# Splitting the scaling of the second exponentials between VectorE and GpSimd in a differential attention kernel

## The reference

```
Q1, Q2, K1, K2 = halves (64 columns each) of xn @ Wq + bq and xn @ Wk + bk
A1 = Q1 @ K1.T / 8;  A2 = Q2 @ K2.T / 8
P  = softmax(A1) - lam * softmax(A2)        # rows over 1024 keys
O  = P @ V;  Y = concat(O) @ Wo + bo;  layer norm of Y, times 0.2
```

## Time and profile before

| what | value |
|---|---|
| median of 3 runs | 1190.11 us (1189.4 to 1190.41) |
| the profiled execution | 1192.49 us |
| its span, first to last instruction | 1190.7 us |
| mean granted clock of PE | 0.987 |
| busy PE, DVE, ACT, POOL | 95%, 76%, 80%, 83% of the span |
| steps of attention | 256, in 32 items of 8 |

### The profile page before, as it was taken

One profiled execution on the slowest core, in us unless ns is written; L12 is line 12 of the kernel. 1 busy time (PEld: TensorE's weight loads), 2 busy tenths in 40 slices (PEclk: granted clock), 3 DMA queues, 4 the chain that ended last, 5 costly groups with the idle time before them and its releaser, 6 DMA issues.

```text
span 1190.7 us, 27816 instructions
## 1 busy us (share of the span) xinstructions
PE 1135.0 (95%) x9730; PEld 767.3 (64%) x9730; DVE 904.9 (76%) x1573; ACT 952.0 (80%) x1711; POOL 986.1 (83%) x609
## 2 busy tenths in 40 slices
PE   5899999999999999999999999999999999997998
PEld 4666666666666666666666666666666666664797
DVE  8778888888888888888887888888888878873510
ACT  3288888988888988888988888888889888884432
POOL 3599999999999999989888999999989888898000
PEclk9899999999999999999999999999999999997999
DMA  8842122222211222222222211122222221100000
GB/s 202 331 113 62 47 61 61 61 61 61 60 43 38 58 61 55 55 66 55 55 45 54 55 45 32 45 55 55 55 55 55 55 55 44 45 2 1 1 19 18
DMA packets 76439, 71.28 MB, mean 60 GB/s; under 512 B 43380, under 2 KB 65396, under 8 KB 76404
## 3 DMA queue, kind: packets, MB, share of 16 engines
q1 hardware_dynamic: 75396, 70.65, 23.4%
q10 hardware_dynamic: 880, 0.19, 0.1%
q0 software_dynamic: 128, 0.01, 0.0%
HBM read 22.59 MB, written 14.68 MB: 31 GB/s over the span
## 4 chain that ended last, share of the span: by engine, by line
PE 63%; POOL 11%; ACT 11%; issue 7%; DVE 7%; ACTq 0%; DMA 0%; DVEq 0%; SPq 0%; POOLq 0%
PE ps L535 21%; PE ps L567 18%; PE ps L553 10%; ACT work L753 7%; POOL p_mix L448 6%; DVE small L947 4%; PE ps L579 4%; PE ps L489 3%; POOL work L445 3%; PE ps L652 3%; ACT p_mix L753 3%; PE ps L639 2%; PE ps L516 1%; DVE pt L903 1%; ACT pt L766 1%
## 5 line engine op out<-in xcount | busy, mean ns | idle before, releaser
L947 DVE TENSOR_REDUCE small<-ps 128x1 f32<-128x1024 f32 x512 | 614.2, 1220 | 185.6 <-PE ps L535 185.5
L448 POOL TENSOR_TENSOR p_mix<-p_mix,work 128x1024 f32<-128x1024 f32 x256 | 608.9, 2378 | 21.4
L766 ACT ACTIVATE pt<-ps 128x512 f32<-128x512 f32 x512 | 305.5, 597 | 144.0 <-PE ps L553 140.2
L553 PE MATMUL ps<-ident,p_mix 64*128 64x64 f32 x4096 | 353.2, 227 | 7.6 <-POOL p_mix L448 5.8
L445 POOL TENSOR_SCALAR work<-work,small 128x1024 f32<-128x1024 f32 x256 | 307.6, 1201 | 57.2 <-DVE small L972 56.5
L553 PEld LDWEIGHTS ps<-ident,p_mix 64*128 64x128 f32 x4096 | 305.8, 140 | 57.6 <-issue 39.5
L753 ACT ACTIVATE p_mix<-ps,small 128x1024 f32<-128x1024 f32 x256 | 286.5, 1119 | 18.0 <-DVE small L947 18.0
L753 ACT ACTIVATE work<-ps,small 128x1024 f32<-128x1024 f32 x256 | 284.4, 1111 | 0.2
L567 PE MATMUL ps<-pt,v_h 128*64 128x512 f32 x1024 | 249.2, 608 | 0.7 <-ACT pt L766 0.7
L535 PE MATMUL ps<-k_hi,q_hi 64*128 64x512 f32 x512 | 227.7, 445 | 10.8 <-ACT p_mix L753 3.4
L535 PE MATMUL ps<-k_hi,q_lo 64*128 64x512 f32 x512 | 226.4, 442 | 0.0
(11 more groups left out here) (135 smaller groups left out, 1219.3 us busy)
## 6 DMA issues: line engine op xcount, KB each, us to landing
qx_hi<-q_hi SPq DMA_DIRECT2D x64, 256.0 KB, 3.8
qx_lo<-q_lo SPq DMA_DIRECT2D x64, 256.0 KB, 4.7
v_scratch<-pt SPq DMA_DIRECT2D x16, 512.0 KB, 4.9
v_h<-v_scratch SPq DMA_DIRECT2D x32, 256.0 KB, 3.2
w_scratch<-wqk_hi SPq DMA_DIRECT2D x16, 160.0 KB, 1.8
w_scratch<-wqk_lo SPq DMA_DIRECT2D x16, 160.0 KB, 1.9
wqk_hi<-w_scratch SPq DMA_DIRECT2D x16, 160.0 KB, 2.2
wqk_lo<-w_scratch SPq DMA_DIRECT2D x16, 160.0 KB, 2.3
```

Of the source, the lines that this page charges most:

```text
L448: pool.tensor_tensor(e1, e1, e2, ALU.add).then_inc(mix_done, 1)
L553: mm = pe.transpose(pt_ps[:, c * D:(c + 1) * D], p_mix[rows, col:col + P], ident[rows, rows])
L766: act.activation(pt4[:, kb % 2, :, j * P + half * D:j * P + (half + 1) * D], pt_ps.rearrange("p (c q) -> p c q", c=KC), ACT.Copy).then_inc ...
L947: dve.tensor_reduce(neg_max[:, m:m + 1], slot[SLOT[k, s]], AX.X, ALU.max, negate=True)\
```

## The change

POOL scales only columns 256 to 1023 of e2, DVE columns 0 to 255. There is now one scalar to scale with, -lam * l1 / l2, made by the second instruction of `inv_sums`, which reads the first one's result and so waits for it. DVE scales its 256 columns with that scalar right after it and waits for it too; it uses the form of the instruction that also writes the sum of its output to a column (`accum_out`). Nobody reads that sum. POOL's instruction keeps two per-row scalars, of which the second is a column of ones, written once at the start. Before it adds, POOL waits for DVE's part also.

```diff
+DVE_KEYS = 256
...
+        part_sum, one = small[:, 244:245], small[:, 245:246]
...
+            pool.memset(one, 1.0).then_inc(id_ready, 1)
...
-            pool.wait_ge(id_ready, 4)
+            pool.wait_ge(id_ready, 5)
...
                     pool.wait_ge(recip_done, 2 * n)
-                    pool.tensor_scalar(e2, e2, l_inv[:, 2 * km + 1:2 * km + 2], l1_neg[:, km % 4:km % 4 + 1],
-                                       ALU.mult, ALU.mult).then_inc(scaled, 1)
+                    pool.tensor_scalar(e2[:, DVE_KEYS:], e2[:, DVE_KEYS:], l1_neg[:, km % 4:km % 4 + 1], one,
+                                       ALU.mult, ALU.mult)\
+                        .then_inc(scaled, 1)
                     pool.wait_ge(scaled, n)
+                    pool.wait_ge(part_scaled, n)
                     pool.tensor_tensor(e1, e1, e2, ALU.add).then_inc(mix_done, 1)
...
                     dve.reciprocal(l_inv[:, r:r + 2], l_sum[:, l:l + 2]).then_inc(recip_done, 1)
-                    dve.tensor_scalar(l1_neg[:, e:e + 1], l_sum[:, l:l + 1], lam_neg, None, ALU.mult)\
-                        .then_inc(recip_done, 1)
+                    dve.wait_ge(recip_done, 2 * m + 1)
+                    dve.tensor_scalar(l1_neg[:, e:e + 1], l_inv[:, r + 1:r + 2], l_sum[:, l:l + 1], lam_neg,
+                                      ALU.mult, ALU.mult).then_inc(recip_done, 1)
+
+                    part = e2_buf[:, e * S:e * S + DVE_KEYS]
+                    dve.wait_ge(recip_done, 2 * m + 2)
+                    dve.tensor_scalar(part, part, l1_neg[:, e:e + 1], 0.0, ALU.mult, ALU.add, accum_out=part_sum)\
+                        .then_inc(part_scaled, 1)
```

More of the change, by code:

```diff
@@ L154, in build @@
         recip_done = sem("recip_done")
-        scaled, mix_done = sem("scaled"), sem("mix_done")
+        scaled, part_scaled, mix_done = sem("scaled"), sem("part_scaled"), sem("mix_done")
         pt_ready, pt_evac = sem("pt_ready"), sem("pt_evac")
```

## The result

The changed kernel takes 1229.6 us (median of 4 runs, 1227.55 to 1231.41) against 1189.99 before: a ratio of 1.0333, 95% interval 1.0316 to 1.035. The forecast was 1234, range 1207 to 1264. Its profiled execution took 1231.4 us, with a span of 1229.6; the span before was 1190.7, so the two traces differ by 38.9 us.

What follows compares the result with a forecast made beforehand. PE sets the pace, and late DVE work reaches it at the low parts: 30 x (0.80 + 0.73) = 45.9 us, less 2.4 at the end, added to 1190.1 gives 1233.6, rounded to 1234 us; range 1207 to 1264.

Steps and rivals of the forecast that it cites:

- One sign: In the profile after, PE idling ended by the low parts: about 0.7 us, twice an item.
- POOL's relief: POOL's scaling of 768 instead of 1024 columns: 0.27 us saved a step, worth nothing within the attention.
- Rival A: POOL's relief counts and DVE's addition hides in its idle time: faster, 1187.7 us; chance 0.06.
- The 2.4 us at the end: Gain where POOL runs nine steps back to back before the last transposes: 9 x 0.27 us.
- d: Extra DVE time in each step from the serial reciprocal, scalar and 256 columns: 0.75 us, range 0.64 to 1.00.
- The sum's output: Added DVE time for writing the accumulator in each step: 0.08 us, range 0 to 0.20.
- slack: Time before the first row maximum of j = 3 that absorbs DVE's delay: 0.61 + 0.09 = 0.70 us.
- the forecast's own rule: K blocks lose the whole lateness at j = 3, 0.80 us; Q blocks 0.07 less, 0.73 us.
- The sum: Total over 30 items, one Q and one K block each: 45.9 us, less 2.4, so +43.5 us.
- Rival B: DVE's new instruction is cheap, d = 0.53 us: a little slower, 1207 us; chance 0.12.
- rival C: DVE's new instruction is held by POOL's running one, 0.81 us on the mean: 1331 us; chance 0.05.
- Rival D: POOL's scaling turns slow, some 2.2 us for 768 columns, above PE's pace: 1340 us; chance 0.02.

Runs made afterwards that it cites:

- the relief alone: Kernel before, with POOL scaling only columns 256 to 1023 and nobody scaling the first 256: 1187.81 us, ratio 0.9988.
- the plain form: Changed kernel with DVE's 256-column scaling not writing the sum of its output (no accum_out): 1350.32 us, ratio 1.1342.

## Why the prediction was right

- **What bounds the kernel.** PE, held at the low parts. Shown: PE's busy time did not change, and the split at j = 2 and j = 3 alone gives the whole loss. One sign was read too simply: the forecast had 0.7 us of PE idling at each low part; in the change it is 0.66 and 0.43, and 0.2 in each block stands at the projection ahead of it.
- **POOL's relief.** Forecast 0.27 us a step, measured 0.21 (1.20 to 0.99). That it is worth nothing inside the attention is shown by the unchanged blocks with the relief alone. Rival A fell with it. The 2.4 us at the end were sized too high: 9 x 0.21 = 1.9; the run with the relief alone agrees, within an interval that also holds zero. The count was off in its start: from the scaling at 1056.89 to the addition at 1095.26 there are eight steps. The ninth is the one before them, and it belongs to the chain though POOL idles ahead of it:

```profile
1053.26 1.21 POOL L445 TENSOR_SCALAR work<-work,small 128x1024 f32<-128x1024 f32 x1 [1.39 <-DVE small L972]
```

- **What DVE adds.** d was forecast as 0.75 us and is 0.72. The scalar with two per-row operands was taken at 0.22 and is 0.27, at the upper bound. The 256 columns took 0.48, but 0.41 to the next start, as forecast. The sum's output was taken at 0.08 and adds nothing that shows: its read lasts 0.08, and the next instruction starts together with it.
- **Where d lies on the path.** Forecast 2 x 0.75 - 0.70 = 0.80 us late at j = 3. The first row maximum of j = 3 came 4.43 us after that of j = 2 before and 5.12 to 5.13 after, 0.69 to 0.70 late: 2 x 0.72 less 0.74 of slack. The slack is 0.61, as read, and 0.13 where 0.09 was taken: from the start of `add_y` to the second reciprocal it was 1.17 us before (316.38 to 317.55) and 1.04 after (345.51 to 346.55). In Q blocks the loss is 0.67, where 0.73 was forecast, in K blocks 0.66, where 0.80 was. The forecast had K blocks lose more than Q blocks; they don't. Over items 4 to 29 the row maximum of j = 3 is 0.70 late in both. Q blocks get 0.03 back behind it, where 0.07 was forecast; K blocks get 0.04 back between the block's start and the row maximum of j = 2 and 0.01 behind j = 3, where nothing was. Why is open, and that the two add up to the 1.33 of the forecast's own rule (0.70 + 0.63) is luck.
- **The sum.** 30 x 1.33 = 39.9 us and some 1.9 less at the end would be 38, against 45.9 - 2.4 = 43.5; measured are 39.6 in the medians and 38.9 in the spans. The error is two terms sized 0.03 (d) and 0.04 us (the slack) off, each counted 60 times or more.
- **The second row maximum at j = 1.** The forecast said that it delays the projection ahead of a longer hold. Shown: alone it costs 8.5 us, beside the other nothing.
- **Rival B** (a cheap instruction, d = 0.53) fell by the measured d, **rival C** by durations of 478 to 482 ns; C is what the plain form does, and its price of 1331 us was low by 19. That it came so near is luck in part: C put a mean hold of 0.81 us on each of the two parts ahead of the row maximum of j = 3, and the runs have 0.03 and 1.60 beyond the free 0.36, which happens to be the same sum. It has no term for POOL's slower scaling or PE's lower clock. **Rival D**: POOL's scaling stayed fast.

## What to carry to other kernels

Look at what an added instruction stands in front of in its own queue, not at the engine's busy share: with DVE idle for 9 us in 50, 0.7 us more was free at j = 0, and 0.7 more at both j = 2 and j = 3 cost 0.67 us a block; moving the columns behind the urgent work gave 28 of 40 us back. Relief for an engine pays only where that engine is waited for, here in the last eight steps. Before giving DVE work from SBUF to SBUF beside a busy GpSimd, measure whether the form is held.

## What the hardware showed that was not expected

- DVE's scaling with the sum is slower alone and much faster beside POOL than the plain form: 0.48 against a mean of 0.87 us for 256 columns. The Trainium skill (SBUF — State Buffer, Who interferes with whom) names both sides of it, and both traces agree: 478 to 482 ns for the form that it exempts, up to 2454 for the other.
- POOL's scaling with two per-row scalars took 1.20, 0.99, 0.77 and 0.55 us for 1024, 768, 512 and 256 columns: 0.85 ns a column and 0.33 us. The form with one per-row scalar and one multiplication took 1.55 us for 512 columns. Why the form with two of each is cheaper was not looked into.
- A DVE instruction of one column with two per-row operands and two multiplications took 0.27 us, 0.08 more than one with one of each (0.19). The second operation is not what costs: with constants as operands, instructions of one column took 0.14 us with one operation and 0.13 with two (at 38.95 and 39.01 us of the trace before).
